# Attention with its softmax sums inverted on ScalarE, x transposed three tiles ahead, and the query bias added on VectorE

## The reference

```python
qh = _split_heads(q @ wq_w + wq_b, b, sq)      # q is the layer-normed x; 16 heads of 16
kh = _split_heads(k @ wk_w + wk_b, b, sk)
vh = _split_heads(v @ wv_w + wv_b, b, sk)
logits = jnp.einsum('bhqd,bhkd->bhqk', qh, kh) / jnp.sqrt(jnp.float32(DEPTH))
logits = logits + mask * NEG_BIG
attn = jax.nn.softmax(logits, axis=-1)
out = jnp.einsum('bhqk,bhkd->bhqd', attn, vh)
return out.transpose(0, 2, 1, 3).reshape(b, sq, D_MODEL) @ wo_w + wo_b
```

## Time and profile before

| | |
|---|---|
| median of 3 runs | 1198.31 us (1197.46 to 1198.68) |
| the profiled execution, its own time | 1199.42 us |
| its span | 1197.7 us |
| PE busy | 1024.8 us, 86% of the span |
| DVE busy | 855.8 us, 71% |
| ACT busy | 560.2 us, 47% |
| POOL busy | 491.8 us, 41% |
| granted TensorE clock, mean | 0.959 of full |

### The profile page before, as it was taken

One profiled execution on the slowest core, in us unless ns is written; L12 is line 12 of the kernel. 1 busy time (PEld: TensorE's weight loads), 2 busy tenths in 40 slices (PEclk: granted clock), 3 DMA queues, 4 the chain that ended last, 5 costly groups with the idle time before them and its releaser, 6 DMA issues. The chain is left out here.

```text
span 1197.7 us, 24813 instructions
## 1 busy us (share of the span) xinstructions
PE 1024.8 (86%) x9211; PEld 795.3 (66%) x9226; DVE 855.8 (71%) x1867; ACT 560.2 (47%) x1104; POOL 491.8 (41%) x494
## 2 busy tenths in 40 slices
PE   0779999999479999999999977999999967888886
PEld 0657776777368888888888865777777743444443
DVE  0747777777666666676676575777777756888886
ACT  0245555555343333333333244555555535777775
POOL 0134444444213322332233322444444427999991
PEclk9969999999779999999999997999999987999999
DMA  9300000000000000000000040000000000000000
GB/s 322 60 1 2 2 2 2 2 2 2 1 1 1 0 0 0 0 0 0 0 0 0 1 137 1 2 2 2 2 2 2 2 1 1 23 24 25 23 23 27
DMA packets 19420, 20.97 MB, mean 18 GB/s; under 512 B 6528, under 2 KB 17920, under 8 KB 19072
## 3 DMA queue, kind: packets, MB, share of 16 engines
q1 hardware_dynamic: 17712, 19.12, 5.2%
q10 hardware_dynamic: 1616, 0.58, 0.3%
HBM read 15.51 MB, written 4.19 MB: 16 GB/s over the span
## 5 line engine op out<-in xcount | busy, mean ns | idle before, releaser
L398 POOL TENSOR_TENSOR sm_a<-sm_a,mx_a 128x616 f32<-128x616 f32 x128 | 153.2, 1218 | 282.2 <-DVE mx_a L565 282.2
L666 POOL TENSOR_TENSOR hl_f<-hf_f,hh_f 128x512 fp32r<-128x512 f32 x80 | 103.6, 1295 | 262.4 <-ACT hh_f L790 262.4
L530 ACT ACTIVATE pt_a<-pT_a 128x512 f32<-128x512 f32 (+1 forms) x192 | 101.0, 528 | 175.7 <-PE pT_a L453 175.5
L558 DVE TENSOR_TENSOR sm_a<-pS_a,mask 128x616 f32<-128x616 f32 x128 | 101.1, 791 | 43.8 <-PE pS_a L439 43.8
L689 PE MATMUL pGU_f<-xh_f,wgh_f 128*128 (+1 forms) x320 | 128.7, 402 | 0.0
L785 ACT ACTIVATE sg_f<-pGU_f 128x512 f32<-128x512 f32 x80 | 47.9, 599 | 170.1 <-PE pGU_f L691 170.0
L691 PE MATMUL pGU_f<-xh_f,wgl_f 128*128 (+1 forms) x320 | 125.3, 392 | 0.0
L690 PE MATMUL pGU_f<-xl_f,wgh_f 128*128 (+1 forms) x320 | 125.3, 392 | 0.0
L896 DVE TENSOR_TENSOR hf_f<-pGU_f,sg_f 128x512 f32<-128x512 f32 x80 | 55.4, 692 | 90.7 <-ACT sg_f L785 90.7
L906 DVE SCALAR_TENSOR_TENSOR x<-pD_f,coef_f,x 128x256 f32 (+1 forms) x256 | 106.2, 477 | 18.3 <-PE pD_f L728 16.8
L570 DVE RECIPROCAL rc_a<-pO_a 128x256 f32<-128x256 f32 x64 | 111.9, 1748 | 8.6 <-PE pO_a L467 8.6
(11 more groups left out here) (182 smaller groups left out, 2273.8 us busy)
## 6 DMA issues: line engine op xcount, KB each, us to landing
x<-x_in SPq DMA_DIRECT2D x4, 1024.0 KB, 14.0
out_x<-x SPq DMA_DIRECT2D x32, 128.0 KB, 1.7
gu<-gu_in SPq DMA_DIRECT2D x1, 2560.0 KB, 15.5
aw<-aw_in SPq DMA_DIRECT2D x2, 1024.0 KB, 11.6
w<-w_in SPq DMA_DIRECT2D x2, 1024.0 KB, 6.5
dn<-dn_in SPq DMA_DIRECT2D x1, 1280.0 KB, 14.6
b<-b_in SPq DMA_DIRECT2D x1, 512.0 KB, 9.4
g<-g_in SPq DMA_DIRECT2D x1, 512.0 KB, 10.2
```

The source lines that it names most:

```text
L398: pool.tensor_tensor(heads, heads, mx[u][:, g, :].rearrange("p (h a) -> p h a", a=1).broadcast_to([P, HG, SK]), ALU.subtract).then_inc(shi ...
L530: act.activation(pt[u][:, lo:lo + n, :].rearrange("p n t -> p (n t)"), pT[:, (J * t + j) % 2, 0:n * P], ACT.Copy).then_inc(pt_sb, 1)
L558: dve.tensor_tensor(sm[u][:, g, :].rearrange("p (b h k) -> p b h k", b=2, k=SK), pS[:, 2 * g:2 * g + 2, 0:HS].rearrange("p b (h k) -> p b ...
L666: pool.tensor_tensor(hl[u][:], hf[u][:], f32(hh[u][:]), ALU.subtract).then_inc(hl_ok, 1)
```

## The change

Three things, all in `attention_phase`:

1. The inverse of the sums. `reciprocal` on DVE is replaced by ACT's `inverse`: rc = exp(-ln(sums)). DVE's `refine` then makes one Newton step: rf = sums * rc, rc = (rf - 2) * rc, which is the inverse with its sign turned; `normalise` multiplies the values by -1 and by rc. `inverse(t - 1)` stands first in ACT's step, ahead of `pt_out(t, 0)`. On DVE `refine`, `normalise` and the new `q_out` stand between the two `largest`, which stood together before.
2. x is transposed three tiles ahead instead of two: `turn_x(t + 3)` stands behind `project(t - 1)` on PE, `xt_out(t + 3)` between the two `exp` on ACT, and `norm` runs four tiles ahead. The pipeline begins one step earlier. `turn_x` also waits for `q_sb` of the tile before.
3. The query bias: `q_out` goes from ACT (two activations) to DVE (one addition over both halves).

```diff
--- before.py
+++ after.py
@@ -361,9 +361,9 @@
         sem = lambda n: ctx.enter_context(nc.semaphore(n + tag))
         sbt = lambda n, s, d=F32: ctx.enter_context(nc.sbuf_tensor(n + tag, s, d))
         pst = lambda n, s, d=F32: ctx.enter_context(nc.psum_tensor(n + tag, s, d))
-        (padded, normed, xt_ps, xt_sb, q_ps, q_sb, scored, masked, maxed, shifted, exped, pt_ps, pt_sb,
+        (padded, logged, refined, normed, xt_ps, xt_sb, q_ps, q_sb, scored, masked, maxed, shifted, exped, pt_ps, pt_sb,
          weighed, recips, o_norm, projected, biased, added, stated) = (sem(n) for n in (
-             "padded", "normed", "xt_ps", "xt_sb", "q_ps", "q_sb", "scored", "masked", "maxed", "shifted",
+             "padded", "logged", "refined", "normed", "xt_ps", "xt_sb", "q_ps", "q_sb", "scored", "masked", "maxed", "shifted",
              "exped", "pt_ps", "pt_sb", "weighed", "recips", "o_norm", "projected", "biased", "added", "stated"))
         NS = HG * SK
         HS = NS // 2
@@ -371,6 +371,7 @@
         J = -(-len(chunks) // 4)
         pair = lambda n, s: [sbt(f"{n}{i}", s) for i in range(2)]
         xn, xt, q, ot, rc = (pair(n, [P, D]) for n in ("xn", "xt", "q", "ot", "rc"))
+        rf = sbt("rf", [P, D])
         sm = pair("sm", [P, G, NS])
         mx = pair("mx", [P, G, HG])
         pr = pair("pr", [P, G, CK * P])
@@ -416,6 +417,7 @@
             def turn_x(t, u):
                 pe.wait_ge(normed, t + 1)
                 count(pe, xt_sb, t)
+                count(pe, q_sb, t)
                 for k in range(G):
                     mm = pe.transpose(pA[:, k * P:(k + 1) * P], xn[u][:, k * P:(k + 1) * P], sb["ident"][:])
                 mm.then_inc(xt_ps, 1)
@@ -479,9 +481,6 @@
             def step(t, u, has):
                 if has(0):
                     turn_p(t, u, 0)
-                if has(2):
-                    turn_x(t + 2, u)
-                if has(0):
                     turn_p(t, u, 1)
                 if has(2):
                     queries(t + 2, u)
@@ -489,12 +488,14 @@
                     turn_p(t, u, 2)
                 if has(-1):
                     project(t - 1, 1 - u)
+                if has(3):
+                    turn_x(t + 3, 1 - u)
                 if has(2):
                     scores(t + 2, u)
                 if has(0):
                     weigh(t, u)
 
-            lay_out_steps(step, 3, 1)
+            lay_out_steps(step, 4, 1)
 
         @block.scalar
         def _(act):
@@ -507,14 +508,6 @@
                 act.wait_ge(xt_ps, t + 1)
                 count(act, q_ps, t - 1)
                 act.activation(xt[u][:], pA[:, 0:D], ACT.Copy).then_inc(xt_sb, 1)
-
-            def q_out(t, u):
-                act.wait_ge(q_ps, t + 1)
-                count(act, scored, G * (t - 1))
-                for g in range(G):
-                    last = act.activation(q[u][:, g * P:(g + 1) * P], pA[:, D + g * P:D + (g + 1) * P], ACT.Identity,
-                                          bias=bqkv[:, 0, g:g + 1])
-                last.then_inc(q_sb, 1)
 
             def exp(t, u, g):
                 act.wait_ge(shifted, G * t + g + 1)
@@ -530,24 +523,29 @@
                 act.activation(pt[u][:, lo:lo + n, :].rearrange("p n t -> p (n t)"),
                                pT[:, (J * t + j) % 2, 0:n * P], ACT.Copy).then_inc(pt_sb, 1)
 
+            def inverse(t, u):
+                act.wait_ge(weighed, t + 1)
+                act.activation(rc[u][:], pO[:, D:2 * D], ACT.Ln).then_inc(logged, 1)
+                act.wait_ge(logged, t + 1)
+                act.activation(rc[u][:], rc[u][:], ACT.Exp, scale=-1.0).then_inc(recips, 1)
+
             def step(t, u, has):
+                if has(-1):
+                    inverse(t - 1, 1 - u)
                 if has(0):
                     pt_out(t, u, 0)
-                if has(2):
-                    xt_out(t + 2, u)
-                if has(0):
                     pt_out(t, u, 1)
-                if has(2):
-                    q_out(t + 2, u)
-                if has(0):
                     pt_out(t, u, 2)
                 if has(1):
                     exp(t + 1, 1 - u, 0)
+                if has(3):
+                    xt_out(t + 3, 1 - u)
+                if has(1):
                     exp(t + 1, 1 - u, 1)
-                if has(3):
-                    norm(t + 3, 1 - u)
-
-            lay_out_steps(step, 3, 1)
+                if has(4):
+                    norm(t + 4, u)
+
+            lay_out_steps(step, 4, 1)
 
         @block.vector
         def _(dve):
@@ -565,12 +563,24 @@
                 dve.tensor_reduce(mx[u][:, g, :], sm[u][:, g, :].rearrange("p (h k) -> p h k", k=SK),
                                   AX.X, ALU.max).then_inc(maxed, 1)
 
+            def q_out(t, u):
+                dve.wait_ge(q_ps, t + 1)
+                count(dve, scored, G * (t - 1))
+                dve.tensor_tensor(q[u][:].rearrange("p (g n) -> p g n", g=G),
+                                  pA[:, D:2 * D].rearrange("p (g n) -> p g n", g=G),
+                                  bqkv[:, 0, :].rearrange("p (g a) -> p g a", a=1).broadcast_to([P, G, P]),
+                                  ALU.add).then_inc(q_sb, 1)
+
+            def refine(t, u):
+                dve.wait_ge(recips, t + 1)
+                dve.tensor_tensor(rf[:], pO[:, D:2 * D], rc[u][:], ALU.mult).then_inc(refined, 1)
+                dve.wait_ge(refined, 2 * t + 1)
+                dve.scalar_tensor_tensor(rc[u][:], rf[:], -2.0, rc[u][:], ALU.add, ALU.mult).then_inc(refined, 1)
+
             def normalise(t, u):
-                dve.wait_ge(weighed, t + 1)
-                dve.reciprocal(rc[u][:], pO[:, D:2 * D]).then_inc(recips, 1)
                 count(dve, projected, t - 1)
-                dve.wait_ge(recips, t + 1)
-                dve.tensor_tensor(ot[u][:], pO[:, 0:D], rc[u][:], ALU.mult).then_inc(o_norm, 1)
+                dve.wait_ge(refined, 2 * t + 2)
+                dve.scalar_tensor_tensor(ot[u][:], pO[:, 0:D], -1.0, rc[u][:], ALU.mult, ALU.mult).then_inc(o_norm, 1)
 
             def add(t):
                 dve.wait_ge(projected, t + 1)
@@ -588,9 +598,14 @@
             def step(t, u, has):
                 if has(1):
                     largest(t + 1, 1 - u, 0)
+                if has(-1):
+                    refine(t - 1, 1 - u)
+                    normalise(t - 1, 1 - u)
+                if has(2):
+                    q_out(t + 2, u)
+                if has(1):
                     largest(t + 1, 1 - u, 1)
                 if has(-1):
-                    normalise(t - 1, 1 - u)
                     add(t - 1)
                 if has(2):
                     mask(t + 2, u, 0)
```

## The result

| | before | after |
|---|---|---|
| median of the runs | 1197.92 us (1197.46 to 1198.68) | 1271.49 us (1261.63 to 1274.1) |
| ratio | | 1.060, 95% interval 1.055 to 1.064 |
| the profiled execution, its own time | 1199.42 us | 1261.63 us |
| its span | 1197.7 us | 1259.9 us |

A forecast was written before the change was run, and what follows sets the result against it. A chain through PE and DVE bounds the kernel at 7.45 us a tile; afterwards Ring A at 8.62. 31 x 1.17 plus 1.45 is 37.7 a layer, 75.4 on 1199.42 gives 1274.8, less 1.1: 1274 us, range 1256 to 1310.

The forecast's parts named there:

- The falls: Drops of the granted clock to the 1.2 GHz level when PE idles twice in close succession; 1.2 us each.
- Ring A: Cycle through DVE, POOL and ACT holding both table loads, closing one tile later; 8.62 us, the longer, hence the period.
- Chain B: Cycle through PE: inverse on ACT, Newton step on DVE, projection, transpose, scores, weighing; 8.32 us; alone setting the period, 1255 us.
- The 37.7 us a layer: Time added per attention layer: 31 intervals at 1.17 us, 36.3, plus 1.45 at its end; 75.4 for two.
- The 1.45: Extra time from a layer's last weighing to `ot`: 3.79 us where it was 2.34.
- The price of a load: Each table load on ACT takes 1.28 us, counted as 1.29 with the step ahead; two in each attention tile.
- The rival of 1448 us: Rival: a table switch costs 2.66 us, both standing in Ring A, for a period of 11.38 us; chance 0.04.
- Faster: Rival: no table load in the attention loop, Chain B at 7.03 us then the bound, 1173 us; chance 0.03.
- The granted clock: Rival: PE's two waits lower the clock in every fourth tile (1293 us), second (1311) or all (1348); chance 0.22.
- my case: Ring A sets the attention period, with Chain B alone as the lower end; 1255 to 1285 us, chance 0.67.
- (c): x transposed a tile earlier removes PE's wait for `xt`; worth nothing, since PE would only wait longer for `ot`.
- the 0.87 us: In the old tile chain the reciprocal starts 0.87 us after the weighing ends, DVE being still in `largest`.

The follow-up runs named there:

- last two experiments: The kernel before with only the inverse changed, both `largest` ahead of it: 1284.88 us; the same with POOL's `bias` waiting for `ot` of the tile before: 1271.26 us.
- one moved line: The kernel before with only the second `largest` moved behind `normalise` on DVE: 1167.99 us, ratio 0.975.
- with the transposes first: The kernel before with the second `largest` behind `normalise`, plus `turn_x` first in PE's step and `xt_out` first in ACT's: 1157.26 us, ratio 0.966.
- the two runs in which the DVE instruction is slow: The changed kernel with both `largest` ahead of the Newton step: 1307.55 us; the kernel before with only the inverse changed, both `largest` first: 1284.88 us.
- the inverse alone: The kernel before with logarithm, exponential and Newton step for the reciprocal, both `largest` ahead of it, nothing else changed: 1284.88 us, ratio 1.072.

## Why the prediction was right, and where it was not

The time, 1274 against 1271.49, was met within 3 us. Two errors of opposite sign made it so, and that is luck: the sum was of a ring without falls, and with PE kept busy that ring measures 1256, 18 below it. The falls, which the sum left to a rival, bring 15 to 20 us back. Point by point:

- **Which chain bounds: right.** "Ring A sets the period" is shown twice, by the timeline that closes after 8.43 and by the period falling to 8.15 when the Newton step leaves the ring. Chain B was forecast at 8.32 and measures 8.15.
- **Ring A, 8.62: too large by 0.19.** Its DVE part, from the end of the exponential to the end of `largest`, takes 2.46 us (193.68 to 196.14) where 2.65 stood. I had taken `scalar_tensor_tensor` at 0.473, its form with a pointer; with constants it takes 0.424, and there are two (0.10). The hand-over from ACT to DVE is 0.03 for 0.06, and from the first to the second Newton instruction 0.03 for 0.10 (0.10). POOL's part and ACT's part agree within 0.02. Over 62 intervals 0.18 is 11 us.
- **The 37.7 us a layer: too large also at its ends.** 31 x 1.17 on top of what it was is 266.2 and 265.6 us from the first to the last `ot`; without falls it is 258.84 and 258.83. Of the 7.4 and 6.7 between, 5.6 each are the period (31 x 0.18). The other 1.8 and 1.1 are the last four intervals, 8.15 to 7.28, which the sum counted like the rest. The first of them has no `norm` left in ring A; the logarithm then waits 0.2 for the weighing, and 8.15 is chain B's time. In the second, x is no longer transposed between projection and scores, and in the last two there are no scores of a later tile. The 1.45 on the way from a weighing to its `ot` measures 1.27 in the last tile (3.62 for 2.35, each to the end of `ot`). By the sum the fill takes as long as before, within 1 us, so that the first `ot` would come 1.45 later; it comes 2.1 us earlier (84.32 for 86.45), and the first of the second layer follows the last of the first layer after 434.9 us for 435.8. All of this together is some 8 us beside the 11.
- **The price of a load: right.** 1283 ns each, 128 of them; the load ends at 199.99 and the logarithm starts at 200.00. The drain of the Trainium skill ("ScalarE: Activation LUTs", "What ACT_TABLE_LOAD costs") is not seen: in the attention phases the next activation starts within 0.02 us of the load's end wherever it has nothing else to wait for. The rival of 1448 us is out.
- **Faster: out.** Its condition, no load in the loop, is what the copy in place of the logarithm made: period 6.88 where the rival said 7.03. The time, 1156.5, lies 17 us below the rival's 1173; 9 of it are the period (62 x 0.15), the rest lies in the ends of the layers and the fill (first `ot` at 81.83). The Trainium skill's rule that a logarithm and an exponential share one set ("ScalarE: Activation LUTs", "Table sets: the hidden batching unit") did not hold in this program: each tile has both loads.
- **The granted clock: the rival came true in part.** I priced a fall at 1.2 us; it costs 1.34. I gave it 0.22, and priced it for every fourth tile or more. It happens in every sixth to every fifteenth, in a number that differs from execution to execution. The step that failed is "my case" being a case without falls: the waits of PE that the prediction itself had worked out (it said 0.8 and 0.7; they are 1.09 and 0.52) are enough for it at times.
- **(c), x transposed earlier, worth nothing: true where it was weighed, not beyond.** Per tile it brings nothing with the reciprocal (6.96 with it and the query bias on DVE, 6.97 with neither), but the first `ot` comes 3.8 us earlier (81.89 for 85.69), where the sum had the fill at near nothing. With the inverse on ACT, the wait for `xt` is 1.75 us a tile if x is transposed only two tiles ahead (last two experiments).
- **What I left out: the 0.87 us.** I saw it as a term of the old chain and let it go with the reciprocal. It belongs to the order of two instructions on DVE and can be had without the rest, 0.48 us a tile of it.

Open stays why one execution has four of the long intervals and another ten. Nothing was tried on that, only that with PE busy the profiled execution has none.

## What to carry to other kernels

Moving work to an engine that is half idle is priced by what that engine must do around it: 0.80 us of activations for a reciprocal of 1.75 looks like a gain, and the two table loads beside them, 2.57 us a tile, made it a loss of 6%. When an engine stands ready and the operation that the chain needs comes late by most of a microsecond, look first at what stands ahead of it in its own queue; one moved line gave 2.5% here, and with the transposes first 3.4%. Where a change opens waits on PE, price the clock's falls apart from the sum, and look at the spread of the runs as well as at one profile.

## What the runs showed of the hardware that was not expected

**A VectorE instruction with both inputs in SBUF is held up by a GpSimd instruction that starts with it.** 0.42 us becomes 1.01, while POOL's takes its usual 0.73. In the kernel with the copy for the logarithm the same instruction starts into the last part of a POOL instruction and loses nothing (POOL runs until 122.64):

```profile
121.42 1.22 POOL L399 TENSOR_TENSOR sm_a<-sm_a,mx_a 128x616 f32<-128x616 f32 x1 [1.83 <-DVE mx_a L563]
...
122.48 0.43 DVE L578 SCALAR_TENSOR_TENSOR rc_a<-rf_a,rc_a 128x256 f32<-128x256 f32 x1
```

The first Newton product, which reads one input from PSUM, runs at 0.43 inside the same POOL instruction. Between the two extremes lie five tiles of the run with the inverse alone, in which POOL's instruction starts 0.14 to 0.40 us ahead; the one on DVE then takes 0.86 to 0.61 us. One of them:

```profile
85.27 0.73 POOL L405 TENSOR_TENSOR x<-x,bo 128x256 f32<-128x256 f32 x1
...
85.67 0.62 DVE L581 SCALAR_TENSOR_TENSOR rc_a<-rf_a,rc_a 128x256 f32<-128x256 f32 x1
```

In all 104 tiles of the two runs in which the DVE instruction is slow it ends 0.28 us after POOL's. So it does not go slower: it waits, and then takes its 0.42, as if POOL let go some 0.14 us before its recorded end (an estimate, 0.42 less 0.28). The Trainium skill has the rule for this ("SBUF — State Buffer", "SBUF: two separate sides"): a VectorE operation with two SBUF inputs and a GpSimd operation that reads SBUF exclude each other for the whole instruction, and whichever starts first has the port. The rows agree, but for that last 0.14 us. The wait doesn't show among the waits, it shows only as a longer instruction.

**How often the clock falls differs from execution to execution.** The same kernel took 1261.6 to 1276.7 us, with the same 8.44 us in each undisturbed tile; with 12 transposes a tile that nobody reads it took 1255.5 to 1258.7.
